# Bump attention in a two-layer decoder: one of four tiles of every second head's distances computed by VectorE instead of ScalarE, with a new order of all queues

## The reference, cut to what matters

```python
q_proj = q.reshape(B, T, H * D) @ Wproj.T
k_proj = k.reshape(B, T, H * D) @ Wproj.T
# out_i = sum_j max(0, 1 - |z_i - z_j| / b_h) * v_j,   b_h = softplus(log_bandwidth) + 1e-4
...
ctx = jnp.take_along_axis(ctx_sorted, inv_idx[..., None], axis=2)[:, :, T:]
ctx = ctx / jnp.asarray(T, ctx.dtype)
```

## Time and profile before

| | |
|---|---|
| median of 3 runs | 1278.37 us |
| the profiled execution | 1285.95 us, of which the span of the trace is 1284.1 us |
| PE, DVE, ACT, POOL busy | 1029.0, 774.9, 640.3, 390.5 us |
| ACTIVATEs of L1320 | 256: 16 heads x 4 tiles x 4 sequences |
| hats, L1366 | 64 |
| bump blocks (lane 0's first head to lane 1's last hat) | 175.1 to 268.4 us, and 766.7 to 863.2 us |

### The profile page before, as it was taken

How to read it: one execution, slowest core, us unless ns; L and a number is a source line. 1 busy time by engine, 2 the same in 40 slices (tenths; PEclk the granted TensorE clock), 3 DMA queues, 4 the chain that set the end, 5 groups by cost and what they waited for, 6 DMA issues and landing times. The chain is left out here.

```text
span 1284.1 us, 20213 instructions
## 1 busy us (share of the span) xinstructions
PE 1029.0 (80%) x7286; PEld 598.3 (47%) x7286; DVE 774.9 (60%) x2021; ACT 640.3 (50%) x1252; POOL 390.5 (30%) x773
## 2 busy tenths in 40 slices
PE   6858767878689869589887887787779879859996
PEld 6745322234334469444455431333334459834454
DVE  2854676677796540487445558786788542289443
ACT  2114359854327536327652459783416636415752
POOL 4032111233214531514412211424224432433410
PEclk8878868798789979879998887897979969979998
DMA  8023000111430036550012200012160025462011
GB/s 287 39 67 64 11 1 1 53 32 37 110 101 3 10 127 196 162 128 4 29 50 68 69 12 1 10 50 59 61 145 5 3 97 188 123 176 40 3 36 48
DMA packets 70873, 86.67 MB, mean 67 GB/s; under 512 B 18765, under 2 KB 59005, under 8 KB 70270
## 3 DMA queue, kind: packets, MB, share of 16 engines
q1 hardware_dynamic: 67862, 80.70, 22.1%
q0 software_dynamic: 2048, 4.20, 1.1%
q10 hardware_dynamic: 864, 0.48, 0.1%
HBM read 55.90 MB, written 28.86 MB: 66 GB/s over the span
## 5 line engine op out<-in xcount | busy, mean ns | idle before, releaser
L1571 DVE TENSOR_REDUCE sb_rmax<-banks 128x1 f32<-128x512 f32 (+3 forms) x352 | 206.5, 636 | 70.2 <-PE banks L1419 69.5
L1500 ACT ACTIVATE sb_arena<-banks 128x512 f32<-128x512 f32 x320 | 175.9, 595 | 107.5 <-PE banks L1430 105.8
L1417 PE MATMUL banks<-sb_arena,sb_qs 128*128 128x384 bf16 (+3 forms) x512 | 131.4, 329 | 43.8 <-DMA sb_arena<-k_scratch 25.1
L1320 ACT ACTIVATE sb_arena<-banks,sb_zk 128x512 f32<-128x512 f32 x256 | 152.9, 726 | 23.9 <-PE banks L1270 14.4
L1526 POOL TENSOR_SCALAR_AFFINE_SELECT sb_arena<-sb_arena 128x256 f32<-128x256 f32 x256 | 99.1, 407 | 182.5 <-ACT sb_arena L1500 181.5
L1430 PE MATMUL banks<-sb_qs,sb_arena 128*128 128x384 bf16 (+3 forms) x512 | 108.9, 305 | 12.3 <-DVE sb_rmax L1571 3.7
L480 POOL TENSOR_SCALAR sb_var<-sb_mv 128x4 f32<-128x4 f32 x40 | 14.1, 354 | 331.5 <-DVE sb_mv L465 331.4
L1054 ACT ACTIVATE sb_arena<-banks 77x512 f32<-77x512 f32 x128 | 72.8, 589 | 69.9 <-PE banks L967 49.3
L1366 DVE TENSOR_SCALAR sb_arena<-sb_arena,sb_bw 128x2048 f32<-128x2048 f32 x64 | 86.0, 1354 | 27.6 <-ACT sb_arena L1320 27.5
L1417 PEld LDWEIGHTS banks<-sb_arena,sb_qs 128*128 128x128 bf16 x512 | 47.8, 104 | 103.1 <-DVE sb_rmax L1571 38.6
L1419 PE MATMUL banks<-sb_trib,sb_identb 128*128 128x128 bf16 (+2 forms) x352 | 92.3, 262 | 0.0
(11 more groups left out here) (353 smaller groups left out, 2151.5 us busy)
## 6 DMA issues: line engine op xcount, KB each, us to landing
sb_arena<-in_chosen SPq DMA_DIRECT2D x28, 514.0 KB, 4.5
sb_qs<-q_scratch SPq DMA_DIRECT2D x32, 288.0 KB, 5.0
q_scratch<-sb_region SPq DMA_DIRECT2D x16, 384.0 KB, 2.5
sb_arena<-k_scratch SPq DMA_DIRECT2D x16, 288.0 KB, 7.2
sb_qs<-in_chosen SPq DMA_DIRECT2D x8, 514.0 KB, 5.4
sb_w<-in_w SPq DMA_DIRECT2D x2, 2048.0 KB
q_scratch<-sb_region SPq DMA_DIRECT2D x16, 256.0 KB, 2.2
done<-sb_arena SPq DMA_DIRECT2D x28, 128.0 KB, 5.0
```

The lines of the kernel that those rows point to most:

```text
L1320: i = nc.scalar.activation(L.dist[h % 3][:, kb, :], (b2_, b3)[h % 2], ACT.Abs, bias=L.zk[:, kb, h:h + 1])
L1417: nc.tensor.matmul(o[:, i * kl:(i + 1) * kl], L.qs[:, h // 2, t * 128:kl], L.ks[:, key_of(h), 0:kl], start=(i == 0), stop=False)
L1500: nc.scalar.activation(L.probs[:, u % SLOTS, :], bank_of(SELF_ORDER, ring, ("key", u)), ACT.Exp)\
L1571: nc.vector.tensor_reduce(L.rmax[:, t, g * GROUP + h0:g * GROUP + h0 + nh], bank_of(SELF_ORDER, ring, ("max", step))[:, 0:nh * kl] .rearra ...
```

## The change

For odd heads, ACT computes three key tiles instead of four. DVE computes the fourth in two instructions: the sum zq + (-zk) out of PSUM into the head's buffer (`raw`, 128x512), and, later, the absolute value as a bitwise AND with 0x7FFFFFFF on the same 512 columns seen as int32, just ahead of the hat. ACT's three tiles of an odd head now wait for `raw`, that is for DVE's sum to be done, and DVE's sum takes over the waits for `spread` and `pv`. The AND waits for the sum (`raw`), and the hat of the odd head waits for the AND (`dve_chain`). In a lane DVE's list for two heads is now: sum(h), hat(h - 1), AND(h), hat(h). 32 of 256 ACTIVATEs go, 64 DVE instructions of 128x512 come.

```diff
             for h in range(H):
                 yield
-                act.wait_ge(*p.at("spread", h + 1))
-                if h >= 3:
-                    act.wait_ge(*p.at("pv", h - 2))
-                for kb in range(T):
+                if h % 2:
+                    act.wait_ge(*p.at("raw", h // 2 + 1))
+                else:
+                    act.wait_ge(*p.at("spread", h + 1))
+                    if h >= 3:
+                        act.wait_ge(*p.at("pv", h - 2))
+                for kb in range(T - h % 2):
                     i = nc.scalar.activation(L.dist[h % 3][:, kb, :], (b2_, b3)[h % 2], ACT.Abs,
                                              bias=L.zk[:, kb, h:h + 1])
...
-            for h in range(H):
-                yield
+            def hat(h):
                 dve.wait_ge(*p.at("dist", h + 1))
                 nc.vector.tensor_scalar(L.dist[h % 3], L.dist[h % 3], bw[:, 1, h:h + 1], bw[:, 1, h:h + 1],
                                         ALU.min, ALU.subtract).then_inc(L.sem("hat"), 1)
+            for h in range(1, H, 2):
+                o = L.dist[h % 3][:, T - 1, :]
+                yield
+                dve.wait_ge(*p.at("spread", h + 1))
+                if h >= 3:
+                    dve.wait_ge(*p.at("pv", h - 2))
+                nc.vector.tensor_scalar(o, (b2_, b3)[h % 2], L.zk[:, T - 1, h:h + 1], None, ALU.add)\
+                    .then_inc(L.sem("raw"), 1)
+                yield
+                hat(h - 1)
+                yield
+                dve.wait_ge(*p.at("raw", h // 2 + 1))
+                dve_chain(nc.vector.tensor_scalar(o.bitcast(I32), o.bitcast(I32), 0x7FFFFFFF, None, ALU.bitwise_and))
+                hat(h)
...
 ORDER = {
     "SP":
-    "2855d923e00ff901fe5606c2bf80fd5660063bc7f801ff807f5581b0afe03f55998",
+    "2855d923e00ff901fd5606a2bf80fea660067f43f801ff8077cb81a8afe03f95998",
```

More of the change, by code:

```diff
@@ L159 @@
     "BU": {**_LN, "turned": 1, "ft": 1, "k": 1, "k32": 1, "q": 1, "q32": 1, "q_split": 1, "v": 1, "values": 1,
-           "filled": 1, "spread": H, "dist": H, "hat": H, "pv": H, "osb": G, "y": 1, "res": 1},
+           "filled": 1, "spread": H, "raw": H // 2, "dist": H, "hat": H, "pv": H, "osb": G, "y": 1, "res": 1},
     "S0": {**_SELF, "k_edged": EDGES, "x5": 1},
@@ L183 @@
-    "ffffeff7effdfffffc04540006aa4a90a32244ca854c1292619c9c494925244700c5effff7dfdfffffeefffd10a0001eaaaa"
-    "fffffc008540005d24a90a32244ca854c1292619c9c494925244700c5effffdefffffffddfeb50281ffffc",
+    "803783cf270000004de3fc787e00e0018038001c6effffffefffef1442025210f06d55fb7fe032480140016f6cf6c4aa3424"
+    "068020000696ffffffbf5ff7fffff01150001aa92a428c89132a15304a49867271252494911c0317bfffddff7ffff7dfffea"
+    "2300007aaaabfffff0022a0007ff2d44b5428cc555438aaaac4a49d2984a4a4929318f80cb5efffffefdffe8240aafea7c01"
@@ L185 @@
+    "002014000000fe0f007e000637efffff7f7ffffffbd290809444306cabdbfe26604f80240001fd866db4d44a060060000a55"
+    "ffffeddf7ffffffffc0025400015710a925421455491049d2384a4a4929231e02aadfffefeff7fffbfbffffa88c0001eaaaa"
+    "fffffc008a8001ffaaa22515492583370555a9292694c9e0124ca488fc05ecbefffff7fbfffa048153fffc",
     "ACT":
-    "c03cd9001ffe00f804040c1dffffbe9240240df3003ff10fff01c530080dffefdfc0001ffffe0000fe04995494a52520306f"
-    "fefbffff2000f6affe00003ffff800003f80a529529450083bff7f7ffe7c87ea00304420ffc00007eefbfffdf402240de400"
@@ L188 @@
-    "ffc5a41ffe00e0007bff760000ffffffff800003f80a529529450083bfdfdfffffc8003dabff80000ffffe00000fe0294a54"
-    "a514020effbf7fff9f10ffe",
+    "c03cd9001ffe00f804040c1dffffbe9280a262efc801f8dff8038aa0080bffb7e0000ffffffe00000fe0294a54a514020eff"
+    "7f7ffffe8800f6affe00003ffff8007f02aa9955291545480707dffdffe825fe00082ffe0000000fbffdf7ffd29028916f90"
+    "03fe1ffe001c930005ff40000fffffffff8000003f811515494a0305ff7f7fffffa2003dabff80000ffffe0007f029555549"
+    "454a2a0307bffdfffa047fe",
     "POOL":
-    "81e38b8b601bcf80003fffe0001ffc001cc3199c30c000ffbffffff00ff8008001fffffe000007ff001cc199870c003f7fff"
@@ L192 @@
-    "ffff81a3a73e00cfe60003fffe000007ff001cc199870c003f7ffdedffe0ff8008001fffffe000007ff001cc199870c003f7"
-    "fffffff98",
+    "81e38b8b60378f80003fffe000007ff001cc199870c003f7ffdb6fff0ff8008001fffffe0007ff00e30ccce30cc30c003ffb"
+    "ffff81c7745e0378ec0003fffe0000003ff8009e19867000fdfff6db7ff8ff8008001fffffe0007ff001c333319c30c3000f"
+    "fefffff98",
     "DVE":
-    "003f00fe1f8b80005be000001ffffffff80299d8d2a07074d8b90888a29a8019ffe4e10003ef6de6dffff8c3f01aaa000fea"
-    "ad555557527fff5806ff868407900d4a801ab55aaaad6aafffe65c3f9403d41000000001e6be5ef57fffff0356a34a939b45"
@@ L197 @@
-    "d104449141264207f0003fdde73bfdfffff80fe20352a006ad56aaab5aabfff99703ff868407900d4a801ab55aaaad6aafff"
-    "e65c3f541fe",
+    "003f00fe1f8b80005be000001ffffffff80299d8c462350c6af9b6ab80a11550079e7332640003e7b79bdffff817e20352a0"
+    "06ad56aaab5aabfff99703ff868407901aa5003feed6d5aaaa5557ff805fd0327800056000001ffcfaffffff8066f2c46232"
+    "8a4bcd72bca85091a2019ccf33260007aaf9bdedbfff0f1a101aaa00d5aaaaadaabfffea5d83ff868407901aa5003fed56b5"
+    "5556955fff805fc81fe",
 }
```

4 lines of the change are left out of this document (removed).

## The result

The changed kernel takes 1297.5 us (median of 4 runs, 1296.2 to 1305.9); the kernel before, in the same comparison, 1280.2 us (1278.3 to 1288.6). The ratio of the two sets of runs is put at 1.0148, with a 95% interval of 1.0110 to 1.0186 (the medians alone give 1.0136): 1.5% slower. The forecast was 1275.0 us with a range to 1290: wrong in sign, and outside the range.

A forecast was written before the change was run, and what follows sets the result against it. The prediction took ACT to set the bump block's pace, PE close behind. Each block gives 4.6 - 2.4 - 0.5 = 1.7 us, two give 3.4, other stages 0: from 1278.37 to 1275.0 us, range 1262 to 1290.

The forecast's parts named there:

- What bounds the block: First bump block: ACT sets the pace, busy 79.40 of 90.05 us, PE close behind; DVE idles 25.5 us.
- Sum and AND: DVE's added instructions per pair of heads: 0.69 + 0.43 = 1.12 us, 17.9 us a block, 35.8 in all.
- The walk through the first block: Hand-worked instruction lists: DVE 77.7 us work plus 7.8 idle, last hat at 263.8 us; net block gain 1.7 us.
- the 9.5 us that the prediction named: DVE's idle time in a bump block above which the change gives nothing there; 7.8 us was expected.
- The step that failed: Second bump block: moving some 10 us of lane 1's DVE work ahead makes it like the first, gaining 1.7 us.
- behind the block 2.4 us: Stage behind the first block: half of the 4.7 us of row maxima moved there counted as paid again.
- The other stages get new interleavings: Stages outside the bump blocks: same instructions in new order, taken as 0 with 6 us to either side.
- The check that the prediction set: Stages S0 to M1, no instruction changed: a length difference over 3 us a pass would show the zero term wrong.
- The slower rival: Bump blocks: ACT's wait for DVE's sum replaces the old wait, DVE idles 15 to 16 us; 1289 us, chance 0.27.
- GpSimd beside the AND: Bump blocks: if GpSimd slows 3 of 16 ANDs by 1.1 us, 3.3 us a block; left out of the sum.
- the 6.6 us: Both bump blocks: extra time if GpSimd's shared interfaces slow the ANDs, giving 1281.6 us; not in the forecast.
- the faster rival: Bump blocks: DVE's idle time takes nearly all added work, each block gives 6.0 us; 1266 us, chance 0.23.

The follow-up runs named there:

- sum_behind_act: Changed work in the old order, but on odd heads ACT does its three tiles first and DVE's sum follows, against the kernel before: 1.0189.
- sum_early: Changed kernel in its new order, each DVE sum moved to right behind the odd hat before it, against the kernel before: 1.0227.
- old_work_mid_old: Kernel before with the new order, except the old order from first S0 to end of first-pass M1, against the kernel before: 1.0109.

## Why the prediction was wrong

1. What bounds the block: right. ACT's relief alone gives 0.9923, and the changed block shows DVE fuller than ACT.
2. Sum and AND: 0.742 and 0.452 us for 0.69 and 0.43, inside their bounds; 38.1 us for 35.8, 2.3 us of DVE in all.
3. The walk through the first block: up to its last hat DVE has 76.23 us to do, forecast 77.7 (before's window has 77.67, but it takes in row maxima behind the last hat, so that this agreement is luck); ACT 70.07, forecast 70.0; ACT's wait for L1380 15.8 us, forecast 15. Idle time was 87.60 - 76.23 = 11.4 us, forecast 7.8, so the last hat ended at 265.95 instead of 263.8, and lane 0's residual sum came at 241.6 instead of 238. The idle time is above the 9.5 us that the prediction named as the point where the block gives nothing, and the first block alone measured 1.0028 (1.0003 to 1.0053): about +4 us instead of -1.7.
4. The step that failed: "The new order moves lane 1's steps between 768.49 and 791.93 us ... ahead of the block, which makes it like the first. I count the same 1.7 us." It did make the block like the first: 88.0 us from the first hat to the last, where the first takes 88.1 (177.87 to 265.95 us). What the step left out is that the work moved out of the block has to be done elsewhere. Lane 1's steps now stand ahead of lane 0's first head, and the block begins 11.1 us later. Behind the block DVE has 9 us more to do, and lane 1's X1 needs 8.1 us more there. The prediction took the gain of the block and put the moved work at nothing (behind the block 2.4 us, counted for the first pass). I read the second block's 88% and 79% full engines as lack of room to be cured by moving lane 1's steps out of it; they were full because the block carried other stages' work beside the heads (DVE 76.2 us, where the same heads in the new order leave 61.6). The runs price the step: order of stretch c alone with old work 1.0165, the second block with work and order 1.0165, forecast 0.999.
5. "The other stages get new interleavings ...; I see no row that prices one, take 0, and keep 6 us": a term put at nothing, with 6 us of range, and the order alone costs 17 us (1.0136) over the whole kernel and 30 us (1.0233) in the second pass alone. The check that the prediction set (S0 to M1 differing by over 3 us a pass) came out at +17 and +5 us for the two lanes of the first pass, but that was not the cause: with b put back the marks recovered and the time did not.
6. The slower rival had the right side and the place in part. Its condition, over 9.5 us idle, held; but ACT's wait for the sum isn't the price by itself (sum_behind_act, sum_early), and it foresaw 1289 us from two equal blocks.
7. GpSimd beside the AND: one of 16 in the first block took 1.48 us, and over both blocks the ANDs took 14.5 us for the 32 x 0.42 = 13.4 of undisturbed ones: 1.1 us in all. Other ANDs met GpSimd too and took 0.41 to 0.46 us. The Trainium skill (GPSIMD Engine Reference, key points) has the two engines share interfaces; the slow AND agrees with it, but the 6.6 us that I had worked out by it did not appear. The larger meeting was one that the prediction did not look for, of hats with GpSimd's MEMSET of 2048 columns: two hats took 2.55 and 2.83 us for 1.35, which is about the 2.5 us by which the hats grew.
8. Two slips in the sums, neither of which moves the forecast: the upper bound of sum and AND is 16 x (0.75 + 0.69) = 23.0 us, not 23.1, and the faster rival lets X1's maxima cost nothing but still takes 2.4 us off for them.

Open: how the second pass's loss divides between the lanes' distance and the rest of stretch c; why the work costs 1.0121 there with the old order and adds nothing on top of the new one (the block grows from 94.1 to 108.5 us in the one case, and goes from 90.2 to 88.0 in the other); why the new orders of c and d cost old work 1.0233 behind the old order of a and only 1.0109 behind the new one (`old_work_mid_old`, on another chip); and which part of the bond costs the 11 us, if it is the bond. No version beat the kernel before: its work with the new order in the first block is level (0.9988), and what is faster (0.9923) leaves part of the work out.

## What to carry to other kernels

Where an order is made anew with a change, run the old work in the new order and the new work in the old one first: here the order by itself lost 1.4%, and no reading of the changed instructions could have shown it. Before you move one lane's steps out of a stage with full engines, ask where they will run: here the block of the old work got 3.9 us shorter by it, and the stretch behind it 9.6 us longer. And work moved from a full engine to one that idles isn't paid by its idle time: 40.6 us into 45.8 us of idle time in the two blocks cost 19 us, and the relief of 18.8 us on ACT returned 10.

## What the runs showed of the hardware

An integer AND of 512 columns in SBUF, on fp32 words read as int32, takes 0.42 us, as the fp32 cast of that size. A sum with a column's scalar out of PSUM takes 0.742 us where the copy takes 0.692, and a row maximum of 512 fp32 columns in SBUF 0.676. The AND that ran beside GpSimd's instructions took 1.48 us; on POOL, in its timeline:

```profile
257.22 0.98 POOL L1079 TENSOR_SCALAR sb_mask<-sb_mask 128x308 f32<-128x308 int32 x1
258.17 1.41 POOL L1080 TENSOR_TENSOR sb_nrm<-sb_xall,sb_rows 128x512 f32<-128x512 f32 x1
```

It ends at 259.86 us, 0.3 us after L1080. A hat beside GpSimd's MEMSET of the same size lost more:

```profile
196.63 2.55 DVE L1370 TENSOR_SCALAR sb_arena<-sb_arena,sb_bw 128x2048 f32<-128x2048 f32 x1
```
```profile
196.30 1.81 POOL L1337 MEMSET sb_arena<- 128x2048 f32 x1
```

There the MEMSET began first, and the hat took 2.55 us for 1.35. In the trace of the kernel before the hats at 192.34 us began first, and the MEMSET (194.09 us) took 2.88 us for 1.80: the one that came second paid, in both cases over 1 us.

```profile
194.09 2.88 POOL L1333 MEMSET sb_arena<- 128x2048 f32 x1
```

The granted clock of TensorE's slow stretch changed too: from 220 to 240 us it averages 0.83 now and 0.57 before, with PE busy 15.92 and 19.07 of 20 us. Matmuls take longer at the lower clock, so which of the two made the other isn't shown. The block didn't get faster by it.

```profile
220.00:240.00 20.00, 15.92 (x102) 5.17 (x102) 16.48 (x19) 17.99 (x32) 0.00 (x0) 0.83 0.00 1
```
